# Feature attention on one core: seven tiles' sums sorted by transfers through DRAM instead of selection products

## The reference, cut to what matters

```
def _L3_xattn_ref(q, k, v):              # q is layernorm(x), k and v are the context
    qh = q.reshape(b * h, d // h, m)     # groups of d // h = 8 tokens
    kh = k.reshape(b * h, d // h, -1)
    vh = v.reshape(b * h, c // h, -1)
    qk = jnp.einsum('bdm,bdn->bmn', qh, kh) * scale
    sm = jax.nn.softmax(qk, axis=-1)
    ret = jnp.einsum('bmn,bcn->bcm', sm, vh)
    return ret.reshape(b, c, m)
```

## Time and profile before

| | |
|---|---|
| median of 3 runs | 1135.2 us |
| span of the profiled execution | 1132.8 us |
| TensorE busy, mean granted clock | 1032.7 us (91%), 0.950 |
| VectorE, ScalarE, GpSimd busy | 565.9, 367.3, 265.6 us |
| chain that ended last: TensorE, VectorE, ScalarE, DMA | 76%, 12%, 5%, 3% |
| DMA | 67.25 MB, mean 59 GB/s |

### The profile page before, as it was taken

One profiled execution on the slowest core, in us unless ns is written; L12 is line 12 of the kernel. 1 busy time (PEld: TensorE's weight loads), 2 busy tenths in 40 slices (PEclk: granted clock), 3 DMA queues, 4 the chain that ended last, 5 costly groups with the idle time before them and its releaser, 6 DMA issues.

```text
span 1132.8 us, 17516 instructions
## 1 busy us (share of the span) xinstructions
PE 1032.7 (91%) x6658; PEld 691.2 (61%) x6658; DVE 565.9 (50%) x1286; ACT 367.3 (32%) x687; POOL 265.6 (23%) x336
## 2 busy tenths in 40 slices
PE   5979999989999999988865799999959999997989
PEld 4766699446767676757645577777723434453467
DVE  5876423534434343446466221221257787657792
ACT  3562233232121212213311121221204566735660
POOL 5421431500000000003431222222152453302350
PEclk9995999999999999999895999999976999998999
DMA  9003032211011010057017102111010400020000
GB/s 290 25 2 103 19 97 86 84 43 29 22 31 38 25 38 5 11 197 262 1 33 283 33 28 72 69 33 42 14 66 19 157 1 1 2 75 1 0 6 33
DMA packets 37432, 67.25 MB, mean 59 GB/s; under 512 B 4456, under 2 KB 27080, under 8 KB 35816
## 3 DMA queue, kind: packets, MB, share of 16 engines
q1 hardware_dynamic: 29960, 51.98, 13.5%
q0 software_dynamic: 4080, 11.15, 3.5%
q10 hardware_dynamic: 3312, 3.02, 0.8%
HBM read 54.72 MB, written 11.40 MB: 58 GB/s over the span
## 4 chain that ended last, share of the span: by engine, by line
PE 76%; DVE 12%; ACT 5%; DMA 3%; issue 2%; POOL 2%; SPq 0%; DVEq 0%; ACTq 0%; POOLq 0%
PE bank L354 22%; PE bank L1269 12%; PE bank L1293 7%; PE bank L1619 6%; PE bank L2340 5%; PE bank L2365 3%; PE bank L2386 3%; PE bank L1629 3%; PE bank L1282 2%; PE bank L1604 2%; PE bank L2835 2%; PE bank L1594 2%; PE bank L2404 1%; DVE big L2622 1%; DMA big<-yg,big 1%
## 5 line engine op out<-in xcount | busy, mean ns | idle before, releaser
L1269 PE MATMUL bank<-big 128*128 x552 | 147.7, 418 | 0.6 <-ACT big L1154 0.6
L354 PE MATMUL bank<-XNT,big 128*128 128x512 f32 x296 | 137.9, 615 | 7.1 <-DVE big L2575 5.6
L1269 PEld LDWEIGHTS bank<-big 128*128 128x128 f32 x552 | 98.3, 192 | 39.2 <-issue 2.5
L270 POOL TENSOR_TENSOR rstd<-ve,half 128x1 f32<-128x1 f32 x48 | 27.8, 584 | 330.5 <-DVE ve L264 330.2
L2340 PE MATMUL bank<-big,xs 32*128 32x512 f32 x256 | 89.9, 739 | 11.6 <-DVE xs L281 10.1
L354 PEld LDWEIGHTS bank<-XNT,big 128*128 128x128 f32 x296 | 55.8, 196 | 70.8 <-issue 59.9
L2195 DVE TENSOR_REDUCE big<-bank 128x2 f32<-128x512 f32 x128 | 82.0, 685 | 21.1 <-PE bank L2340 20.4
L1293 PE MATMUL bank<-big 128*128 (+1 forms) x368 | 87.2, 380 | 1.1 <-ACT big L1169 1.1
L1047 DVE TENSOR_TENSOR big<-big,bank 128x704 f32<-128x704 f32 x23 | 20.4, 889 | 124.6 <-ACT big L1162 124.6
L2286 ACT ACTIVATE big<-bank 128x1024 f32<-128x1024 f32 x64 | 64.9, 1024 | 40.2 <-PE bank L2365 39.9
L354 PE MATMUL bank<-CTXT,big 128*128 128x512 f32 (+1 forms) x192 | 67.0, 494 | 11.0 <-DMA big<-wvT 11.0
(11 more groups left out here) (350 smaller groups left out, 1803.2 us busy)
## 6 DMA issues: line engine op xcount, KB each, us to landing
big<-m_gu SPq DMA_DIRECT2D x8, 1408.0 KB
big<-m_d SPq DMA_DIRECT2D x8, 768.0 KB
big<-a_qk SPq DMA_DIRECT2D x16, 256.0 KB, 2.9
yg<-big ACTq DMA_DIRECT2D x23, 128.0 KB, 2.1
big<-m_gu SPq DMA_DIRECT2D x8, 352.0 KB
big<-a_o SPq DMA_DIRECT2D x16, 128.0 KB, 2.0
xn<-XNT SPq DMA_DIRECT2D x8, 256.0 KB, 6.0
big<-f_keys SPq DMA_DIRECT2D x1, 2048.0 KB, 9.2
```

The source lines that it names most:

```text
L270: e.tensor_tensor(k.rstd[at % NT][:, :], k.ve[at % NT][:, :], k.half[:, 0:1], ALU.pow).then_inc(k.ln_rstd, 1)
L354: ins = e.matmul(out, a, b, start=start and n == 0, stop=stop and n == len(pairs) - 1)
L1269: ins = e.matmul(out, xgT[s % 2][:, kb, :], WB[:, bass.ds(at[s] + (kb * 2 * F + c * chunk), chunk)], start=kb == 0, stop=kb == KB - 1)
```

## The change

For tiles 0 to 6 `sort` and `sorted_out` are gone. SP stores the two halves of `vs` to a DRAM buffer `rows6` and, after both have landed, loads two halves of `od` from it; the order of the dimensions does the sorting. `inverse` waits for these loads. Tile 7 keeps the products. Within each strip the values and the ones are laid out anew (`places`: three smaller memsets in the place of two, and another target of the copies), and the selection matrices with them. The wait of `turned` for `od` goes, and with it that of `sort` for the exponentials. The six weight loads of the last stage move from behind the x of layer 6 to the start of SP's list in the feature attention, after a wait that TensorE is through with the layer before.

```
+    rows_out = k.dram["rows6"].rearrange("t r q j x d -> t j (r q) x d")
+    rows_in = k.dram["rows6"].rearrange("t r q j x d -> t q r (j x) d")
...
+    def sp(e):
+        front = k.front.get(7)
+        if front:
+            e.wait_ge(y_ps, y_all)
+            front["load"](e)
+        for t in range(NT - 1):
+            after(e, "vs", t + 1)
+            if t > 0:
+                after(e, "v_sb", t)
+            for jp in (0, 1):
+                e.dma_start(rows_out[t, jp], vs[:, jp * D:(jp + 1) * D]).then_inc(S["row"], 16)
+            after(e, "row", 64 * t + 32)
+            for part in (0, 1):
+                e.dma_start(od[:, part * D:(part + 1) * D], rows_in[t, part]).then_inc(S["row"], 16)
...
-                ins = e.tensor_copy(places(t % 2)[:, kb * G:(kb + 1) * G, j, 2 * G * j:2 * G * j + G], src[:, :, j])
+                ins = e.tensor_copy(places(t % 2)[:, kb * G:(kb + 1) * G, j, G * j:G * j + G], src[:, :, j])
...
         def inverse(t, half):
-            after(e, "od", t + 1)
+            if t < NT - 1:
+                after(e, "row", 64 * (t + 1))
+            else:
+                after(e, "od", 1)
...
         def sums(t):
             after(e, "v_ps", UNITS * (t + 1))
             if t > 0:
-                after(e, "o_ps", t)
+                after(e, "row", 64 * t - 32)
...
-            if u % UNITS == 1 and t > 0:
-                sorted_out(t - 1)
...
-                if u % UNITS == 2 and t > 0 and pair == B_:
-                    after(e, "od", t)
...
-                if u == LAST and t > 0:
-                    after(e, "od", t)
...
-            if u % UNITS == 1 and t > 0:
-                sort(t - 1)
...
+    def load(e):
+        for dst, src in ((wq, g["p7_q"]), (keys, g["p7_keys"]), (wgu, g["p7_gu"]), (de, g["p7_de"]),
+                         (ue, g["p7_ue"]), (dn, g["p7_dn"])):
+            e.dma_start(dst, src).then_inc(S["ld"], 16)
...
     def sp(e):
-        e.wait_ge(k.x_tile, LOADED + 8 * min(l, 6))
-        for dst, src in ((wq, g["p7_q"]), (keys, g["p7_keys"]), (wgu, g["p7_gu"]), (de, g["p7_de"]),
-                         (ue, g["p7_ue"]), (dn, g["p7_dn"])):
-            e.dma_start(dst, src).then_inc(S["ld"], 16)
+        if l < 6:
+            e.wait_ge(k.x_tile, LOADED + 8 * l)
+            load(e)
...
+                    rows6=nc.dram_tensor("rows6", (NT, 4, 2, 2, 16, D), F32, kind="Internal").ap(), out=out)
```

More of the change, by code:

```diff
@@ L2050, in feature_attention @@
     TB, SBK, SBN, VB = 0, 4, 3, 7
-    NTB, OB = TB + 2, TB + 3
+    NTB, RB = TB + 2, SBK + SBN - 1
     A_, B_ = 0, 1
     at0, done0 = 8 * l, LOADED + 8 * l
-    masks0 = k.count_masks(10)
+    masks0 = k.count_masks(14)
     A, B = Arena(k.big[:, 3384:16200], 16200 - 3384), Arena(k.late, 8800)
@@ L2067, in feature_attention @@
     S, start = k.again(names)
-    for n in ("tm", "less", "sel"):
+    for n in ("tm", "less", "sel", "row"):
         S[n], start[n] = k.sem("f6_" + n), 0
-    k.f6_out, k.f6_out_at = S["od"], start["od"] + NT
+    k.f6_out, k.f6_out_at = S["od"], start["od"] + 1
+    rows_out = k.dram["rows6"].rearrange("t r q j x d -> t j (r q) x d")
+    rows_in = k.dram["rows6"].rearrange("t r q j x d -> t q r (j x) d")
     if l >= 6:
@@ L2104, in maxima_bank @@
         return spare_bank(UNITS * t - 2, NTB)
-    def result_bank(t):
-        return spare_bank(UNITS * (t + 1) + 1, OB)
     def spare_bank(u, b):
@@ L2164, in pool @@
             for j in (0, 1):
-                e.memset(places(p)[:, :, j, 2 * G * (1 - j):2 * G * (2 - j)], 0.0).then_inc(k.masks, 1)
-                e.memset(places(p)[:, :, j, 2 * G * j + G:2 * G * j + 2 * G], 1.0).then_inc(k.masks, 1)
+                e.memset(places(p)[:, :, j, G * (1 - j):G * (2 - j)], 0.0).then_inc(k.masks, 1)
+                e.memset(places(p)[:, :, j, 2 * G + G * (1 - j):2 * G + G * (2 - j)], 0.0).then_inc(k.masks, 1)
+                e.memset(places(p)[:, :, j, 2 * G + G * j:2 * G + G * j + G], 1.0).then_inc(k.masks, 1)
         values(0)
@@ L2291, in sums, with sorted_out @@
             if t > 0:
-                after(e, "o_ps", t)
+                after(e, "row", 64 * t - 32)
             e.copy(vs, k.bank[:, VB, :]).then_inc(S["vs"], 1)
[L2295 to L2299, removed]
+        def sorted_out():
+            after(e, "o_ps", 1)
+            after(e, "v_sb", NT - 1)
+            e.copy(od, k.bank[:, RB, :]).then_inc(S["od"], 1)
         maxima(0)
@@ L2325, in act @@
             front["rows"](e, 4)
-        sorted_out(NT - 1)
+        sorted_out()
     def pe(e):
@@ L2390, in values, with sort @@
                 ins.then_inc(S["v_ps"], 1)
[L2392 to L2401, removed]
+        def sort():
+            after(e, "sel", 16)
+            after(e, "vs", NT)
+            after(e, "nm", NT)
             for part in (0, 1):
                 for jp in (0, 1):
-                    ins = e.matmul(bank[:, result_bank(t), part * D:(part + 1) * D], sel[:, 2 * part + jp],
+                    ins = e.matmul(bank[:, RB, part * D:(part + 1) * D], sel[:, 2 * part + jp],
                                    vs[:, jp * D:(jp + 1) * D], start=jp == 0, stop=jp == 1, skip_group_check=True)
@@ L2442, in pe @@
                 front["turn"](e, t)
-        sort(NT - 1)
-    return dict(sp_first=sp_first, pool=pool, dve=dve, act=act, pe=pe, ready=ready)
+        sort()
+    return dict(sp_first=sp_first, sp=sp, pool=pool, dve=dve, act=act, pe=pe, ready=ready)
 def peer_mlp(k, l):
@@ L2516, in front_rows @@
             e.copy(dst[:, :, :, q], src).then_inc(k.xt_sb, 1)
+    def load(e):
+        for dst, src in ((wq, g["p7_q"]), (keys, g["p7_keys"]), (wgu, g["p7_gu"]), (de, g["p7_de"]),
+                         (ue, g["p7_ue"]), (dn, g["p7_dn"])):
+            e.dma_start(dst, src).then_inc(S["ld"], 16)
     if l >= 6:
-        k.front[7] = dict(stats=front_stats, norm=front_norm, turn=front_turn, rows=front_rows,
+        k.front[7] = dict(load=load, stats=front_stats, norm=front_norm, turn=front_turn, rows=front_rows,
                           dve_behind={(2, 0): (("stats", (0, 1)),), (2, 1): (("stats", (2, 3)),),
@@ L2920, in later_layers @@
     for part, jp, r, j, c in itertools.product(range(2), range(2), range(4), range(2), range(8)):
-        sel[part, jp, r, j, part, c, r, jp, j, c] = 1.0
+        sel[part, jp, r, part, j, c, r, jp, j, c] = 1.0
     g["f6_tables"] = sel.reshape(4, P, P).transpose(1, 0, 2)
@@ L2933, in program @@
                     yg=nc.dram_tensor("yg", (TILES * P, D), F32, kind="Internal").ap(),
-                    xd=nc.dram_tensor("xd", (T, D), F32, kind="Internal").ap(), out=out)
+                    xd=nc.dram_tensor("xd", (T, D), F32, kind="Internal").ap(),
+                    rows6=nc.dram_tensor("rows6", (NT, 4, 2, 2, 16, D), F32, kind="Internal").ap(), out=out)
         k = shared(nc, ctx, dram)
         stages = [constants(k)] + [MAKERS[l](k, n) for n, l in enumerate(which)]
-        out_st = k.sem("out_st")
+        out_st = None if "stores" in stages[-1] else k.sem("out_st")
         block = ctx.enter_context(nc.Block())
```

## The result

The changed kernel takes 1153.6 us (median; 1150.9 to 1154.4), the kernel before 1134.5: a ratio of 1.0168, 95% interval 1.0147 to 1.0189. That is 16 us over the forecast and above its range.

A forecast was written before the change was run, and what follows sets the result against it. TensorE, busy in all 17.2 us of a steady tile, was taken as the bound. Five tiles +1.8 us and the end +0.3 gave +2.1 on the 1132.8 span, plus 2.4 to the median: 1137.3 us, range 1125.5 to 1144.

The forecast's parts named there:

- The number of engines: New DRAM transfers: stores on 8 engines, loads on 4, 24 closing packets a tile instead of 64.
- 88-row transfers: Eight `m_d` transfers in the earlier trace: 11 closing packets each, read as the engine count dividing the outermost dimension.
- a tile takes 9.91 + L: Steady attention tiles: 9.91 us from `inverse` to the next `vs`, plus L; five tiles change by +1.8 us.
- L: Latency of the two dependent DRAM passes, from `vs` ready to `od` loaded; forecast 7.70 us.
- the norm as the floor: Steady tiles: with L under 5.94 us VectorE's norm sets the tile, and five tiles gain at most 6.75 us.
- the gain of 1.22 at unit 26: `turned` no longer waits for the copy behind the sort; the last maxima release it 1.22 us earlier.
- the weights at nothing: Last stage's weight loads, issued early on SP: done at 871, before the first `vs`, at no cost.
- the place of the late wait at the end: `turn` of tiles 4 and 5 waits for the norm behind tile 6's `inverse`; last sort 0.3 us later.
- I take 8 and 4 ... L = 7.70 us: Latency from `vs` to `od`: stores on 8 engines 2.95 us, loads on 4 engines 4.69, wake-ups 0.06.
- 48 ns a KB: Packet pace on one DMA engine, from one store alone; used to size the new stores and loads.
- the second rival: Slower transfers hold `inverse` on VectorE, 6 us per us of L: 1143 us at 60 ns a KB; chance 0.3.
- a late `inverse` stops TensorE at once: VectorE's maxima stand behind `inverse`; TensorE runs only three scores ahead, so its wait delays the next tile.
- The four memsets: Extra memsets on GpSimd ahead of the first `less`, normally covered by ScalarE's maxima; put at under 1 us.

The follow-up runs named there:

- the run with the early norm alone: The changed kernel with the norm of tiles 4 and 5 ahead of tile 6's reciprocal in VectorE's list and nothing else: 1149.8 us, ratio 1.0135.

## Why the prediction was wrong

**Right.** The number of engines: 24 closing packets a tile, as forecast from the 88-row transfers, and 80 or 24 when only the outermost counts change. The Trainium skill's page "DMA: Bandwidth & Descriptors", section "Why a DMA increments its semaphore by 16 and not by 1" (the largest divisor up to 16 of both sides' slowest dimension), agrees with all three counts. Right too: the rule "a tile takes 9.91 + L" (9.86 measured at L of 7.40 and 8.92), the norm as the floor under it (15.94 us), the gain of 1.22 at unit 26 (1.17), the weights at nothing, and the place of the late wait at the end.

**Wrong, first: "I take 8 and 4 ... L = 7.70 us".** L is 8.92, 1.22 more. Stores to loads are 3.62 us where 2.98 stood (903.54 to 907.16), the loads to the reciprocal 5.27 where 4.72 stood. Two things were sized too low; how much of the 1.22 us each is worth was not measured by itself. A packet's 48 ns a KB is not the pace of a pass: the 64 KB on each of the four engines ran from about 908.5 to 912.1 in the DMA view, some 56 ns a KB, and the second transfer of a pair is issued 0.6 us after the first. And the landing times of the earlier trace rows are no end of a wait: the stores' last packets lie in the slice that ends at 906.8, SP's next issue is at 907.16; 0.03 us had been put for this. With 5.8 us over five tiles and 1.6 at the end (L was 9.31 there) this is 7.4 us: the second rival's mechanism, whose 1143 us is the time for nearly this L (8.66).

**Wrong, second: "a late `inverse` stops TensorE at once", priced at the wait alone.** That a stopped TensorE loses its clock stands in no term, rival or bound, and it was worth 7.4 us in the profiled execution. In the steady tiles of the kernel before, TensorE does not wait and the clock is 1.00. But the opening of the same stage shows the price: there TensorE waited 2.25 us (until 847.19) and twice some 0.75 us for VectorE's maxima, and the clock, 1.00 from 840 to 843 us, was 0.50 until 867.

```profile
847.00:865.90 18.90, 17.19 (x54) 7.16 (x58) 12.93 (x25) 6.32 (x9) 4.89 (x4) 0.50 0.11 28
```

In the changed kernel four waits of five were followed by 0.50; the run with products in the gaps shows that this is the clock's part: 94.21 us for the five tiles at full clock, where 101.29 had been.

The remaining 1.7 us came ahead of the stage's first sums, 1.55 of it already in the layer before; it lies within the spread between executions. The four memsets were not tried by themselves, but the trace shows no cost: behind them GpSimd still waits 4.27 us for ScalarE, where it waited 4.43.

## What to carry to other kernels

- Before a product is replaced by a transfer, find the instruction that will wait for it, and move that one back by the latency, or move what stands behind it ahead of it: with the same transfers both moves together made the difference between 1.7% slower and 0.6% faster.
- Read the outermost count of both sides of each transfer; counts of 8 and 4 meant so many engines here, by the closing packets. Sum a dependent pass from the issue to the first instruction behind the wait, not to the landing.
- If a change makes TensorE wait in a stretch that was full, price the clock as well as the wait: here the clock cost 7.4 us in five tiles and the wait 7.6. What the clock does behind a wait can often be read elsewhere in the trace of before, as here at the opening of the stage.

## What the hardware showed unexpectedly

- TensorE at 0.50 after waits of about 2 us: 893 to 899 us in the first tile, but not in the next one, after a wait as long (1.95 us, clock 1.00); in the run with the early norm alone it was five of five. Which waits do it stayed open.
- VectorE's sum of two SBUF tiles took 1.72 us instead of 0.41 beside GpSimd's product of 1.89, in each of the four such tiles (1.67 to 1.72), 0.41 in the fifth tile, where no such product runs beside it, and 0.41 to 0.42 where it was moved past it. The Trainium skill's page "Trainium Architecture — The Big Picture", section "What this means for kernel authors", says that the two engines' shared port is an exclusive lock rather than a split of bandwidth; a sum that ends right behind the product agrees with that.
